# Local attention of two small layers: E turned one step later, the maxima subtracted inside ScalarE's exponentials

## The reference, cut to what matters

```python
h = shift_token(x)                       # second half of a token comes from the token before
q, k, v = split(h @ wqkv)
q = l2norm(q) * qs;  k = l2norm(k) * ksc
q, k = rotary_xpos(q, k)                 # rotation and a scale that depends on the position
sim = einsum(q * 8, k of this window and the one before)     # 64 x 128 a head and window
attn = softmax(where(mask, -max, sim))
x = x + (attn @ v) @ wo
h = layernorm(shift_token(x)) * lg + lb
a, g = split(h @ w1 + b1)
x = x + (a * gelu(g)) @ w2 + b2
```

## Time and profile before

| | |
|---|---|
| median of 3 runs | 1146.2 us (1145.76 to 1147.83) |
| the profiled execution | 1146.11 us, span 1144.2 us, mean granted clock 0.978 |
| TensorE busy, share of the span | 1070.0 us, 94% |
| VectorE | 836.6 us, 73% |
| GpSimd | 751.2 us, 66% |
| ScalarE | 632.1 us, 55% |
| chain that ended last, over the two layers | TensorE nearly throughout |

### The profile page before, as it was taken

One profiled execution on the slowest core, in us unless ns is written; L12 is line 12 of the kernel. 1 busy time (PEld: TensorE's weight loads), 2 busy tenths in 40 slices (PEclk: granted clock), 3 DMA queues, 4 the chain that ended last, 5 costly groups with the idle time before them and its releaser, 6 DMA issues. The chain is left out here.

```text
span 1144.2 us, 22954 instructions
## 1 busy us (share of the span) xinstructions
PE 1070.0 (94%) x8344; PEld 665.8 (58%) x8344; DVE 836.6 (73%) x1521; ACT 632.1 (55%) x998; POOL 751.2 (66%) x511
## 2 busy tenths in 40 slices
PE   6884899999999999999999999789999898999988
PEld 4452455555555555555555555756777795777678
DVE  6994666666766666676666663889998689888867
ACT  2442356666666566656655654036666455666554
POOL 3662466767677776867677677389996337666526
PEclk9996799999999999999999999899999999999999
DMA  8899621524215243151242101001111100111111
GB/s 260 275 270 352 155 54 48 111 71 88 75 47 113 48 91 84 50 116 43 75 94 66 48 11 47 10 10 32 42 33 32 26 2 19 32 33 33 34 26 36
DMA packets 82625, 88.48 MB, mean 77 GB/s; under 512 B 32037, under 2 KB 65361, under 8 KB 82513
## 3 DMA queue, kind: packets, MB, share of 16 engines
q1 hardware_dynamic: 82512, 87.01, 29.7%
HBM read 53.04 MB, written 24.24 MB: 68 GB/s over the span
## 5 line engine op out<-in xcount | busy, mean ns | idle before, releaser
L873 DVE CUSTOM_DVE_ANT_0 junk<-psum,alibi 128x1024 bf16<-128x1024 f32 x256 | 313.1, 1223 | 200.7 <-PE psum L929 191.9
L845 ACT ACTIVATE E<-psum,keybias_sb 128x1024 f32<-128x1024 f32 x256 | 274.7, 1112 | 229.0 <-PE psum L953 215.8
L775 POOL TENSOR_TENSOR sum_p<-sum_p,E 128x1024 f32<-128x1024 f32 x96 | 232.4, 2421 | 89.3 <-ACT E L845 84.6
L965 PE MATMUL psum<-E,V 128*64 128x512 f32 x1024 | 248.2, 606 | 0.0
L929 PE MATMUL psum<-KH,QH 64*128 64x512 f32 x512 | 118.8, 459 | 12.8 <-PEq L274 7.3
L965 PEld LDWEIGHTS psum<-E,V 128*64 128x64 f32 x1024 | 62.2, 136 | 112.2 <-issue 98.5
L781 POOL TENSOR_TENSOR sum_p<-sum_p,xpos_sb 128x1024 f32<-128x1024 f32 x32 | 76.3, 2383 | 69.1 <-DVE xpos_sb L883 69.1
L929 PEld LDWEIGHTS psum<-KH,QH 64*128 64x128 f32 x512 | 49.5, 189 | 121.8 <-DVE M L873 84.5
L953 PE MATMUL psum<-QH,KH 64*128 64x512 f32 x512 | 102.3, 395 | 2.1 <-DVE M L873 2.1
L953 PE MATMUL psum<-QL,KH 64*128 64x512 f32 x512 | 101.7, 392 | 0.0
L953 PE MATMUL psum<-QH,KL 64*128 64x512 f32 x512 | 101.6, 392 | 0.0
(11 more groups left out here) (151 smaller groups left out, 2079.3 us busy)
## 6 DMA issues: line engine op xcount, KB each, us to landing
QH<-qa_scratch SPq DMA_DIRECT2D x64, 256.0 KB, 4.2
qa_scratch<-tH SPq DMA_DIRECT2D x8, 1024.0 KB, 5.4
qa_scratch<-tL SPq DMA_DIRECT2D x8, 1024.0 KB, 7.8
QL<-qa_scratch SPq DMA_DIRECT2D x64, 128.0 KB, 4.1
vp_att<-v_att SPq DMA_DIRECT2D x64, 128.0 KB, 2.3
XF<-inverse_scratch SPq DMA_DIRECT2D x30, 256.0 KB, 3.5
KH<-k_scratch SPq DMA_DIRECT2D x16, 256.0 KB, 4.1
KL<-k_scratch SPq DMA_DIRECT2D x16, 256.0 KB, 5.3
```

The lines of the kernel that those rows point to most:

```text
L775: pool.tensor_tensor(sum_p[:, s, :], first, E[:, k % 4, :], ALU.add)\
L845: act.activation(E[:, k % 4, :], scores(k % 2), ACT.Exp, bias=kb).then_inc(exp_done, 1)
L873: dve.tensor_tensor_reduce(junk[:, :], banks(max_bank(i, k), 2), alibi[:, s, :], -1.0, BIG, ALU.add, ALU.min, M[:, s, k:k + 1]).then_inc(m ...
L965: last = pe.matmul(banks(6 + i % 2)[HD * ch:HD * ch + HD, :], V[:, g, k, :], E[:, k % 4, ch * 512:(ch + 1) * 512], start=(k == 0), stop=(k ...
```

## The change

- `shift_scores` and its two matmuls are gone, with their identity matrix. Instead ScalarE takes eight exponentials, one per head over 128 columns, each with the negated maximum of its rows as its bias. The semaphore `exp_done` counts 8 for a tile.
- `turn_e` has the lag PV instead of SCORES: a tile's E is turned in the step after its exponentials, straight after the scores of the next tile. It waits for half of the heads at a time, and for the copies of the next tile's Q and K. `turn_qk` waits for E's copies of two tiles before instead of one.
- `multiply_v` takes the even heads first, then the odd ones.
- The order of the stages changes on TensorE, ScalarE and VectorE.
- The MLP's even tiles use banks 5 and 6, its odd tiles 3 and 4. Its first transpose waits for the exponentials alone, its second for the copies of E.

```diff
         def exponentials(t, s):
-            need(act, shifted, t + 1)
+            need(act, max_done, t + 1)
             need(act, e_turned, 2 * (t - 1))
             need(act, den_done, t - 1)
-            act.activation(E[:, s].rearrange("p h c -> p (h c)"), banks(5, 2), ACT.Exp).then_inc(exp_done, 1)
+            for n in range(FH):
+                act.activation(E[:, s, n, :], banks(5, 2)[:, n * P:(n + 1) * P], ACT.Exp,
+                               bias=nmax[:, s, n:n + 1]).then_inc(exp_done, 1)
...
-        return [(square, NORMS), (take_v, SCORES), (exponentials, SCORES), (take_eT, SCORES), (take_oT, PV),
-                (take_qkT, TURN_QK), (take_hT, TURN_X)]
+        return [(square, NORMS), (take_eT, PV), (exponentials, SCORES), (take_v, SCORES), (take_qkT, TURN_QK),
+                (take_oT, PV), (take_hT, TURN_X)]
...
         def maxima(t, s):
             need(dve, scores_done, t + 1)
-            need(dve, shifted, t - 1)
+            need(dve, exp_done, FH * (t - 1))
...
         def denominators(t, s):
-            need(dve, exp_done, t + 1)
+            need(dve, exp_done, FH * (t + 1))
...
-        return [(maxima, SCORES), (normalise, TURN_QK), (weighted, PV), (square_sums, NORMS), (products, PROJECT),
-                (denominators, SCORES), (residual, OUT)]
+        return [(maxima, SCORES), (normalise, TURN_QK), (square_sums, NORMS), (weighted, PV), (products, PROJECT),
+                (residual, OUT), (denominators, SCORES)]
...
         def multiply_qk(t, s):
             need(pe, qkT_done, 2 * (t + 1))
-            need(pe, exp_done, t)
+            need(pe, exp_done, FH * t)
...
-            for h in range(FH):
+            for h in (*range(0, FH, 2), *range(1, FH, 2)):
                 need(pe, eT_done, 2 * t + slot(h) // 4 + 1)
...
-        def shift_scores(t, s):
-
-            need(pe, max_done, t + 1)
-            for n in range(2):
-                last = pe.matmul(banks(5 + n).rearrange("p (h c) -> p h c", c=P), ident_r[:, :],
-                                 nmax[:, s, 4 * n:4 * n + 4][:, :, None].to_broadcast([P, FH // 2, P]),
-                                 start=False, stop=True, skip_group_check=True)
-            last.then_inc(shifted, 1)
...
         def turn_e(t, s):
-            need(pe, exp_done, t + 1)
-            need(pe, qkT_done, 2 * (t + 1))
+            need(pe, qkT_done, 2 * min(t + 2, T))
             need(pe, eT_done, 2 * t)
             for n in range(2):
+                need(pe, exp_done, FH * t + 4 * (n + 1))
                 for j in range(4):
...
         def turn_qk(t, s):
-                need(pe, eT_done, 2 * (t - 1) + n + 1)
+                need(pe, eT_done, 2 * (t - 2) + n + 1)
...
-        return [(multiply_qk, SCORES), (multiply_v, PV), (project_v, SCORES), (shift_scores, SCORES),
-                (project_qk, PROJECT), (turn_e, SCORES), (turn_o, PV), (turn_qk, TURN_QK), (project_out, OUT),
-                (turn_x, TURN_X)]
+        return [(multiply_qk, SCORES), (turn_e, PV), (project_v, SCORES), (multiply_v, PV),
+                (project_qk, PROJECT), (turn_qk, TURN_QK), (turn_o, PV), (project_out, OUT), (turn_x, TURN_X)]
...
     def ps_x(s):
-        return banks(3 + 2 * s)[:, HC * P:(HC + 1) * P]
+        return banks(5 - 2 * s)[:, HC * P:(HC + 1) * P]
...
-            if t < 2:
-
+            if t == 0:
+                pe.wait_ge(before["exp_done"], FH * T)
+            if t == 1:
                 pe.wait_ge(before["eT_done"], 2 * T)
-                pe.wait_ge(before["exp_done"], T)
```

More of the change, by code:

```diff
@@ L1045, in adaln_block @@
         ident_w = fsb("ident_w", [P, 2, WIN], BF16)
-        ident_r = fsb("ident_r", [P, P], F32R)
         XS = fsb("XS", [P, T, D // 2])
@@ L1095, in _ @@
                 dve.tensor_copy(ident_b[:, :], ident[:, :])
-                dve.tensor_copy(ident_r[:, :], ident[:, :])
                 for w in range(2):
@@ L1105, in adaln_block @@
             att_sems, attention = local_attention(l, psum, sb, new_sem, dict(before), XF, XA, XS, ident, minus_half,
-                                                  fw_qkv, fw_o, xpos[:, l], mask, mask_b, ident_b, ident_w, ident_r)
+                                                  fw_qkv, fw_o, xpos[:, l], mask, mask_b, ident_b, ident_w)
             before.update(att_sems)
@@ L1142, in local_attention @@
 def local_attention(l, psum, sb, new_sem, before, XF, XA, XS, ident, minus_half, fw_qkv, fw_o, xpos, mask, mask_b,
-                    ident_b, ident_w, ident_r):
+                    ident_b, ident_w):
     def banks(a, n=1):
@@ L1168, in local_attention @@
     kT = sb("kT_att", [P, FH // 2, WIN + N])
-    nmax = sb("nmax_att", [P, 2, FH], F32R)
+    nmax = sb("nmax_att", [P, 2, FH])
     E = sb("E_att", [P, 2, FH, 2 * WIN])
@@ L1192, in local_attention @@
     max_done = sem("max_done")
-    shifted = sem("shifted")
     exp_done = sem("exp_done")
@@ L1592, in gelu @@
             for j, n in enumerate(width):
-                act.activation(gate[0:n, s, j, :], banks(3 + 2 * s)[0:n, j * P:(j + 1) * P], ACT.Gelu,
+                act.activation(gate[0:n, s, j, :], banks(5 - 2 * s)[0:n, j * P:(j + 1) * P], ACT.Gelu,
                                bias=fb_1[0:n, l, 1, j:j + 1]).then_inc(gelu_done, 1)
@@ L1626, in gated @@
                 need(dve, gelu_done, HC * t + j + 1)
-                dve.scalar_tensor_tensor(act_in[0:n, s, j, :], banks(4 + 2 * s)[0:n, j * P:(j + 1) * P],
+                dve.scalar_tensor_tensor(act_in[0:n, s, j, :], banks(6 - 2 * s)[0:n, j * P:(j + 1) * P],
                                          fb_1[0:n, l, 0, j:j + 1], gate[0:n, s, j, :], ALU.add, ALU.mult)\
@@ L1654, in hidden @@
                 for j, n in enumerate(width):
-                    last = pe.matmul(banks(3 + 2 * s + m)[0:n, j * P:(j + 1) * P],
+                    last = pe.matmul(banks(5 - 2 * s + m)[0:n, j * P:(j + 1) * P],
                                      fw_1[:, l, off + j * P:off + j * P + n], hT[:, s, :],
```

## The result

| | before | after |
|---|---|---|
| median | 1146.2 us | 1139.1 us (1137.72 to 1140.86) |
| ratio, 95% interval | | 0.9935, 0.9921 to 0.9948 |
| the profiled execution | 1146.11 us, span 1144.2 us | 1139.1 us, span 1137.3 us |
| clock granted over the span | 0.978 | 0.974 |

The change makes the kernel faster by 7.1 us, 0.5 to 0.8%. I had said 16.9, so under half came, and 1139.1 lies just outside my range. The profiled runs differ by 6.9 in their spans, which is what the traces must account for.

What follows compares the result with a forecast made beforehand. TensorE was taken to bound full steps. Layer 1 gains 2.4 + 5.3 + 1.5 = 9.2, layer 0 1.5 less, 7.7; together 16.9, so 1146.1 - 16.9 = 1129.2 us, range 1121 to 1139.

Steps and rivals of the forecast that it cites:

- (b): TensorE's new order: a 0.16 us gap behind short work moves between groups; full step 8.50, bounds 8.37 and 8.7.
- (h): Emptying steps: 17 and 18 save 2.7, step 19 unchanged, step 20 loses 1.2; gain 1.5 us a layer.
- (g): First two steps with scores: gains of 1.7 and 0.7, together 2.4 us a layer.
- (f): GpSimd in layer 0: rstd batches can't be made up at 8.5 a step; charge 1.5 us, bounds 0 and 4.
- a gap at every handoff: Rival on TensorE: three more 0.16 gaps spend the shift's 0.43; only ramps and tails stay, about 1140; chance 0.08.
- (a): Shift's two matmuls leave TensorE's chain: 0.43 us a step, 8.98 becomes 8.55.
- (c): ScalarE: eight exponentials take 2.04 instead of 1.03 us, upper end 3.6; their 7.4 loop stays hidden below 8.5.
- The slower rival: ScalarE: each exponential costs 0.60, 4.8 in all, giving 1176 us; a loss above 0.46 a piece; chance 0.04.
- (d): E turned a step later: costs nothing in full steps; without V's projection as cover, up to 0.6 us.
- (e): VectorE's own work, 8.0 in layer 1 and 8.4 in layer 0, stays under 8.5: costs nothing.
- (i): Swap of banks in the MLP and its two waits: costs nothing.

Runs made afterwards that it cites:

- experiment 6: Kernel after, with O turned ahead of Q and K on TensorE and copied ahead of them on ScalarE: 1142.70 us, ratio 0.9967.
- experiment 8: Kernel before, with the shift gone, eight exponentials, and ScalarE taking them ahead of V's copy: 1136.25 us, ratio 0.9904.
- experiment 5: Kernel after, with Q and K's projection ahead of the products with V on TensorE: 1139.66 us, ratio 0.9935.
- experiment 2: Kernel after, with the old shift and the single exponential put back: 1151.59 us, ratio 1.0041.
- Experiment 1: Kernel before, with only the shift gone and eight exponentials for one, all orders old: 1187.85 us, ratio 1.035.
- experiment 7: Kernel after, with nine idle matmuls (some 1.9 us) in TensorE's wait for the MLP's first tile: 1137.37 us, ratio 0.9919.
- experiment 3: Kernel after, with VectorE's denominators ahead of the residual again: 1133.80 us, ratio 0.9883.
- experiment 4: Kernel after, with TensorE's semaphore waits dropped where an earlier wait already holds them: 1140.44 us, ratio 0.9947.

## Why the prediction was wrong

The step that failed first is (b), TensorE's order. I read two rows, 0.87 for turning E and 1.03 for turning Q and K, as one cost seen from two sides: a gap of 0.16 behind short work. From it I worked out minus 0.16, plus 0.16 and up to minus 0.16, which is 8.39 to 8.55, and took 8.50. But the 1.03 was a wait for a bank (experiments 6 and 8), and the gap that does exist has another rule (experiment 5). By it V's projection gains 0.19, E and Q and K lose 0.15 and 0.19, the bank's wait goes (0.16), and x gets a new wait of 0.18 behind the copy of O: 8.98 - 0.43 - 0.19 - 0.16 + 0.15 + 0.19 + 0.18 = 8.72, against 8.73 measured. My bounds for this step, 8.37 and 8.7, left it out by 0.03. Beside the 8.50 that I took it is 0.23 too long, and in the ledger that is 4.8 of the 10 us that were missing. By itself it would have made 1134; it took the ends (h) and the ramps (g), with 3.9 and 2.5, to come to 1139.1, and GpSimd's charge (f) that wasn't used gave 1.5 back. The rival named for it, a gap at every handoff that leaves 1140, gave nearly the right time by luck: most handoffs show no gap, and half of what was missing lay outside the full steps.

The rest, by the prediction's own steps:

- (a) The shift is worth 0.43 a step: right (experiment 2), once the exponentials are hidden.
- (c) Eight exponentials in 2.04: right. Read like the gelu rows, from the first start to the next instruction's, it is 2.02, one every 0.25 (1017.33 to 1019.35); to the end of the last it is 2.17, where the single one has 1.03. The estimate of 2.35 worked out from the Trainium skill (ScalarE: Activation LUTs, What ACT_TABLE_LOAD costs), which goes by starts too, stands 0.33 above. The slower rival, a price above 0.46 each, didn't come. Experiment 1 shows that a loss had a second way in, ScalarE's order instead of its price, which I hadn't named.
- (d) Turning E later costs nothing in full steps: right, and it wasn't needed (experiment 8). It adds one change from part of the array to the whole, which the sum lacked.
- (e) VectorE costs nothing in full steps: right; its waits moved as I wrote. Where a layer empties it was wrong, see (h).
- (f) GpSimd's charge of 1.5: at most 0.3 of it in the change, as one step of 9.05 right behind the batch of rstd at 809.50, and nothing in the sum of the full steps. At a step of 8.55 it comes, as one of 9.67 at the same place (experiment 6).
- (g) Ramps: 0.77 and 1.48 instead of 2.4 each. In layer 0 half of the miss is the clock: step 4's scores took 1.96, at a clock of 0.79 from 757 to 765, and in experiment 7, whose profiled run has 1.00 and 1.08 there, steps 4 and 5 take 15.53 instead of 16.44. The other half, and all of layer 1's, is the second step, 9.46 in layer 1, where I had taken VectorE's 8.0 for a bound; the chain runs there over VectorE's row from denominators to the weighting of O, with waits of about 1 between.
- (h) Tails: steps 17 and 18 were near 7.2, right. From step 19 on I took a loss of 1.2, for the last E, and it measured 1.33. I had named the denominators between the residual and the MLP's first normalising, and still left step 19 "as it is". They put 1.22 on the chain there, 1.0 a layer more than before, and in layer 0 the clock was lower behind them (1.1), which I hadn't thought of; that the longer wait is the reason is likely, not shown (experiment 7). Moved back, they bring 5.3 (experiment 3).
- (i) The banks: nothing seen.

The trace of before could have shown (b): the end of ScalarE's copy of E beside the start of Q and K's transposes, and the piece of V's projection behind the products with V (1.05) beside its four equal ones for Q and K (1.72, so 0.86 a pair).

## What to carry to other kernels

When two groups of the same matmuls take different times on an unbroken chain, ask for each what ends the difference (a bank, a copy, a change between part of the array and the whole) before it is priced by position; and group matmuls of one tile shape together. When eight small operations replace a large one, the order on their engine decides more than their length: 41 us slower or 10 faster by one swap on ScalarE. An order that is best in full steps needn't be best where a loop empties; a condition on the tile gave 3 us here. And a granted clock read from one trace isn't yet an effect of the change: the same wait had either clock from run to run.

## What the runs showed of the hardware

- Going from a group on part of the array to one on the whole, TensorE lost 0.15 (transposes, 1.02 instead of 0.87) to 0.19 (projections, 1.05 instead of 0.86 and 1.91 instead of 1.72), and 0.2 behind long matmuls on 128x64 (at 707.85 in the kernel after). Why isn't shown.
- Waits on semaphores that were met already cost TensorE nothing that shows (experiment 4).
- After 2.15 us without work TensorE's granted clock over the next six us was 0.61 to 0.74 in six cases and 1.00 in four; with 1.9 us of matmuls in the wait it was 1.00 in both layers.
- Layer 0's first scores took 1.03 to 1.08 in six profiled runs and 1.38 to 1.96 in seven, though TensorE's wait ahead of them was 2.1 in all thirteen; why isn't settled.
- Eight 128x128 exponentials with a bias start 0.25 apart in a row and end 2.17 behind the first start, where one over all 1024 columns takes 1.03.
